# Sums of joined rows in a sandwich of attention and four expert layers: how many there are, and between which instructions they stand

## The reference

```
x = x + LN(attn(LN(x)))       # causal linear attention, 16 heads
x = x + LN(ffn(LN(x)))        # four layers, each as follows
  logits = x @ rw + rb ; the two best of 4 experts, gates that sum to 1
  xe = xhat * g[e] + b[e]     # xhat: x normalized; g, b per expert
  h  = gelu(xe @ w1[e] + b1[e]);  y = h @ w2[e] + b2[e]
  x  = sum over the two experts of gate * (x + y)
```

## Time and profile before

| | |
|---|---|
| median of three runs | 1641.62 us |
| profiled execution | 1646.7 us, its span 1644.9 us |
| PE busy | 1418.8 us (86%) |
| DVE busy | 1274.0 us (77%) |
| ACT busy | 1120.4 us (68%) |
| POOL busy | 847.8 us (52%) |
| attention stage | up to about 403 us |
| layers 0, 1, 2, 3 begin on DVE at | 422, 716, 1017, 1313 us |
| `joined_sums`, L1505 | 100 instructions, 77.8 us |

### The profile page before, as it was taken

The page is one execution under the profiler, slowest core; times in us unless marked ns, Lnnn a source line. Parts: engine busy times, 40 slices in busy tenths (PEclk is TensorE's granted clock), DMA queues, the critical chain, the costliest instruction groups (busy, mean ns, idle before and its releaser), DMA issues.

```text
span 1644.9 us, 36942 instructions
## 1 busy us (share of the span) xinstructions
PE 1418.8 (86%) x11037; PEld 1110.8 (68%) x11037; DVE 1274.0 (77%) x3803; ACT 1120.4 (68%) x1975; POOL 847.8 (52%) x1534
## 2 busy tenths in 40 slices
PE   6999989997779989887999888899989888888882
PEld 4666566667658877666787666678777666766661
DVE  6987888894478887878887877887887888676773
ACT  4443443440858988666898866688988668999871
POOL 2256566765745564234556513355652337787345
PEclk9998998995889999989999998999999899999986
DMA  7963666612858766545786754478766446876532
GB/s 285 397 228 129 260 236 236 269 31 56 222 154 247 229 223 185 179 134 175 208 262 204 216 184 135 131 232 258 233 209 190 141 140 189 206 206 170 168 64 20
DMA packets 181110, 314.11 MB, mean 191 GB/s; under 512 B 37569, under 2 KB 117809, under 8 KB 180529
## 3 DMA queue, kind: packets, MB, share of 16 engines
q1 hardware_dynamic: 159408, 288.27, 55.2%
q0 software_dynamic: 21504, 23.48, 6.2%
HBM read 205.20 MB, written 113.72 MB: 194 GB/s over the span
## 4 chain that ended last, share of the span: by engine, by line
PE 38%; DVE 14%; issue 13%; ACT 7%; POOL 3%; POOLq 0%; ACTq 0%; DVEq 0%
PE ps_h L1817 5%; PE ps_h L1819 5%; PE ps_h L1818 5%; PE ps_q L1850 5%; PE ps_y L1831 5%; PE ps_y L1833 5%; PE ps_y L1832 5%; ACT xh L1373 3%; DVE row L1505 3%; ACT hh L1395 2%; DVE hl L1468 2%; PE ps_t L1804 1%; DVE pbn L1474 1%; DVE row L1533 1%; PE ps_q L1848 1%
## 5 line engine op out<-in xcount | busy, mean ns | idle before, releaser
L1389 ACT ACTIVATE hg<-ps_h,bb 128x512 f32<-128x512 f32 x592 | 389.1, 684 | 225.4 <-PE ps_h L1819 224.4
L1468 DVE TENSOR_TENSOR hl<-hg,hh 128x1024 fp32r<-128x1024 f32 x296 | 360.6, 1220 | 200.2 <-ACT hh L1395 200.0
L1395 ACT ACTIVATE hh<-hg 128x1024 fp32r<-128x1024 f32 x296 | 313.1, 1058 | 3.3 <-PE ps_y L1833 0.9
L1303 POOL DMA_INDIRECT regions<-nrow,posi x192 | 228.9, 1192 | 85.3 <-issue 48.0
L1817 PE MATMUL ps_h<-xTh,w1b 128*128 128x512 f32 x592 | 261.9, 442 | 8.4 <-ACT hg L1389 7.0
L1819 PE MATMUL ps_h<-xTh,w1b 128*128 128x512 f32 x592 | 239.2, 404 | 0.0
L1818 PE MATMUL ps_h<-xTl,w1b 128*128 128x512 f32 x592 | 238.9, 403 | 0.0
L1831 PE MATMUL ps_y<-hh,w2b 128*128 128x512 f32 x592 | 238.8, 403 | 0.0
L1832 PE MATMUL ps_y<-hl,w2b 128*128 128x512 f32 x592 | 236.7, 400 | 0.0
L1833 PE MATMUL ps_y<-hh,w2b 128*128 128x512 f32 x592 | 236.7, 400 | 0.0
L1850 PE MATMUL ps_q<-ir,yb 128*128 128x140 f32 (+2 forms) x888 | 145.6, 298 | 102.0 <-DVE base L1576 61.9
(11 more groups left out here) (277 smaller groups left out, 2652.2 us busy)
## 6 DMA issues: line engine op xcount, KB each, us to landing
w1b<-w_split SPq DMA_DIRECT2D x148, 512.0 KB, 3.7
w2b<-w_split SPq DMA_DIRECT2D x148, 512.0 KB, 4.4
regions<-zero SPq DMA_DIRECT2D x14, 4326.0 KB, 24.6
row<-regions SPq DMA_DIRECT2D x84, 294.0 KB, 4.3
w_split<-wst SPq DMA_DIRECT2D x32, 512.0 KB, 5.1
wr<-in_L_ffn_w_dram SPq DMA_DIRECT2D x32, 256.0 KB, 4.9
regions<-regions SPq DMA_DIRECT2D x24, 294.0 KB
x<-in_L_attn_x_dram SPq DMA_DIRECT2D x16, 256.0 KB, 3.7
```

Source lines behind the costliest of these rows:

```text
L1303: g.indirect_dma_start(out=regions[layer % 2], out_offset=bass.IndirectOffsetOnAxis(ap=posi[r % 2][:, b:b + 1], axis=0), in_=nrow[r % 2][: ...
L1389: a.activation(hg[c // 2 % PAIRS][:, c % 2 * TILE:(c % 2 + 1) * TILE], ps_h[c % BANKS][:], ACT.Gelu, bias=bb[h % BBUFS][:, c % FC:c % FC + ...
L1395: a.activation(hh[j % PAIRS][:], hg[j % PAIRS][:], ACT.Identity).then_inc(hi, 1)
L1468: v.tensor_tensor(hl[n][:], hg[n][:], hh[n][:].bitcast(F32), ALU.subtract).then_inc(lo, 1)
```

## The change

Four edits.

1. `joined_sums` becomes `joined_sum`, one sum at a time, and a tile p takes sums only of the joins q up to p: 15 for a layer in place of 25. `SUM_AT` gives the pair of the layer at which each stands. `update` computes no shares any more: `shares_by_class` stands one pair before it (pair e+3 for tiles with sums).
2. The tables stand further apart: `early_counts` in pair e+9 and `early_tiles` in e+11 of tile 10. In layers 1 to 3 the late ones stand in pairs 9, 11, 13, 15 and 17, in layer 0 in 10, 12, 14, 16 and 18.
3. The folds go on through rounds 7 to 10 with the four experts of layer 1, and POOL adds their `b1` in round 12 (`second_biases`). `later_biases` is left with layers 2 and 3, 32 matmuls.
4. At the end of the attention stage DVE's addition of the later biases stands behind `make_u`, not before it.

```
+SUMS = [(p, q) for p in range(NX) for q in range(p + 1)]
+SUM_AT = [57, 59, 61, 63, 65, 65, 67, 69, 69, 71, 73, 73, 75, 77, 77]
-                return t - 3 if 3 <= t < 3 + E else None
+                return t - 3 if 3 <= t < 3 + 2 * E else None
+                def second_biases():
+                    pool.wait_ge(s_b1x, 2 * E)
+                    g.tensor_tensor(bst[:, E:2 * E, 0:FC], b1x[:, E:], cols[:, K:2 * K].rearrange("p (e c) -> p e c", c=FC), ALU.add).then_inc(s_bias, 1)
...
+                    if t == 12:
+                        second_biases()
...
+                make_u(NT - 1, 3 * NT - 1)
                 dve.wait_ge(s_b1late_ps, 1)
-                v.tensor_tensor(bst[:, E:, 0:FC], ps_b1[:, 0:(L - 1) * K].rearrange("p (n c) -> p n c", c=FC),
-                                cols[:, K:L * K].rearrange("p (n c) -> p n c", c=FC), ALU.add).then_inc(s_bias, 1)
-                make_u(NT - 1, 3 * NT - 1)
+                v.tensor_tensor(bst[:, 2 * E:, 0:FC], ps_b1[:, 0:(L - 2) * K].rearrange("p (n c) -> p n c", c=FC),
+                                cols[:, 2 * K:L * K].rearrange("p (n c) -> p n c", c=FC), ALU.add).then_inc(s_bias, 1)
...
                         pe.wait_ge(s_w1, 16)
+                        if e >= E:
+                            pe.wait_ge(s_w1all, (L - 1) * 16)
+                        weights, at = (w1s, e * F) if e < E else (w1all, (e - E) * F)
...
                 rows_T(NT)
-                later_biases(1)
                 project(NT - 1)
...
-                sp.wait_ge(s_bias, 3)
+                sp.wait_ge(s_bias, 4)
...
-                    dve.wait_ge(t_share, shares[0])
-
-                def joined_sums(n):
+
+                def joined_sum(n, q):

                     p, cols_ = PLACE[n] - FULL, width(n)
-                    dve.wait_ge(p_xh, n + 1)
-                    dve.wait_ge(upd, ROUND0[n])
+                    if q == 0:
+                        dve.wait_ge(p_xh, n + 1)
+                    dve.wait_ge(upd, ROUND0[layer(n) * NU + FULL + q + 1])
+                    link(dve)
                     r = row[n % ROWBUFS]
-                    for q in range(NX):
-                        chained(v.scalar_tensor_tensor(r[:, :, 0:cols_], joined[q][:, :, 0:cols_], belongs[:, q, p:p + 1], r[:, :, 0:cols_], ALU.mult, ALU.add))
-                        link(dve)
+                    chained(v.scalar_tensor_tensor(r[:, :, 0:cols_], joined[q][:, :, 0:cols_], belongs[:, q, p:p + 1], r[:, :, 0:cols_], ALU.mult, ALU.add))
...
                     if part == 0 and gathered(n):
-                        shares_by_class(n)
-                        if main(n):
-                            joined_sums(n)
+                        dve.wait_ge(t_share, shares[0])
+                        link(dve)
...
-                        late = j - START[l * NU] // 2 - (8 if l else 10)
+                        late = j - START[l * NU] // 2 - (9 if l else 10)
...
+                    for l in range(L):
+                        for (tile, q), at in zip(SUMS, SUM_AT):
+                            if at == j - START[l * NU] // 2:
+                                joined_sum(l * NU + FULL + NX + tile, q)
+                    n = ENDS.get(2 * (j - 3))
+                    if main(n) and gathered(n):
+                        shares_by_class(n)
+                    n = ENDS.get(2 * (j - 4))
+                    if joins_in(n if n is not None else -1):
+                        shares_by_class(n)
```

More of the change, by code:

```diff
@@ L93, in sandwich_kernel @@
         base, base_early = sb("base", [P, CL]), sb("base_early", [P, CL])
-        bst, b1x = sb("bst", [P, L * E, FC + 1]), sb("b1x", [P, E, FC])
+        bst, b1x = sb("bst", [P, L * E, FC + 1]), sb("b1x", [P, 2 * E, FC])
         arow = [sb(f"arow{q}", [P, NB, W]) for q in range(AROWS)]
@@ L499, in numbers_and_classes @@
                     g.tensor_copy(base[:], first_row[:]).then_inc(s_consts, 1)
+                def second_biases():
+                    pool.wait_ge(s_b1x, 2 * E)
+                    g.tensor_tensor(bst[:, E:2 * E, 0:FC], b1x[:, E:], cols[:, K:2 * K].rearrange("p (e c) -> p e c", c=FC), ALU.add).then_inc(s_bias, 1)
                 def first_biases():
                     pool.wait_ge(s_b1x, E)
-                    g.tensor_tensor(bst[:, 0:E, 0:FC], b1x[:], cols[:, 0:K].rearrange("p (e c) -> p e c", c=FC), ALU.add).then_inc(s_bias, 1)
+                    g.tensor_tensor(bst[:, 0:E, 0:FC], b1x[:, 0:E], cols[:, 0:K].rearrange("p (e c) -> p e c", c=FC), ALU.add).then_inc(s_bias, 1)
                     g.tensor_copy(bst[:, :, FC:FC + 1], cols[:, B2:B2 + L * E].unsqueeze(2)).then_inc(s_bias, 1)
@@ L816, in transposes @@
                     wait(pe, z_cnt, t - 3)
-                    wait(pe, s_b1x, min(max(t - 3, 0), E))
+                    wait(pe, s_b1x, min(max(t - 3, 0), 2 * E))
                     for b in range(NB):
@@ L859, in logits_and_counts @@
                         pe.wait_ge(s_w1, 16)
+                        if e >= E:
+                            pe.wait_ge(s_w1all, (L - 1) * 16)
+                        weights, at = (w1s, e * F) if e < E else (w1all, (e - E) * F)
                         for c in range(FC):
-                            last = mm(ps_a[:, FOLD.start + c:FOLD.start + c + 1], w1s[:, e * F + c * P:e * F + (c + 1) * P],
+                            last = mm(ps_a[:, FOLD.start + c:FOLD.start + c + 1], weights[:, at + c * P:at + (c + 1) * P],
                                       cols[:, LNB + e:LNB + e + 1], start=True, stop=True)
@@ L865, in later_biases @@
                 def later_biases(l):
-                    if l == 1:
-                        pe.wait_ge(s_w1all, (L - 1) * 16)
+                    if l == 2:
                         pe.wait_ge(a_s, NT * 8)
@@ L872, in later_biases @@
                             at = (n - E) * F + c * P
-                            last = mm(ps_b1[:, (n - E) * FC + c:(n - E) * FC + c + 1], w1all[:, at:at + P],
+                            last = mm(ps_b1[:, (n - 2 * E) * FC + c:(n - 2 * E) * FC + c + 1], w1all[:, at:at + P],
                                       cols[:, LNB + n:LNB + n + 1], start=True, stop=True)
@@ L1730, in _ @@
                         x_rest(n)
-                    if routed(m) and PLACE[m] == EARLY_FROM - 1:
-                        dve.wait_ge(t_base, tile_of(m) + NT + 1)
+                    early = ENDS.get(2 * (j - 9))
+                    if routed(early) and PLACE[early] == EARLY_FROM - 1:
+                        dve.wait_ge(t_base, tile_of(early) + NT + 1)
                         early_counts(dve, base)
-                    early = ENDS.get(2 * (j - 9))
+                    early = ENDS.get(2 * (j - 11))
                     if routed(early) and PLACE[early] == EARLY_FROM - 1:
@@ L1742, in _ @@
                             late_tiles(l)
-                        if late == 1:
+                        if late == 2:
                             joins_of_tiles(l)
-                        if late == 2:
+                        if late == 4:
                             row_parts()
-                        if late == 3:
+                        if late == 6:
                             row_values(0)
-                        if late == 4:
+                        if late == 8:
                             row_values(1)
```

## The result

Four runs of the changed kernel took 1571.57 to 1577.36 us, median 1576.9; four of the kernel before 1640.12 to 1646.62, median 1643.71. The ratio is 0.9587, 95% interval 0.9557 to 0.9618. The profiled execution has a span of 1574.6 us, 70.3 shorter than before. In this table a stretch runs from DVE's `hl` of one pair to that of another, and the last column is the term on record.

What follows compares the result with a forecast made beforehand. Bound: PE's products, with DVE's sums on the path in a loop of PE and DVE. Terms 54.3 - 5.7 + 6.6 + 1.7 + 6.8 - 10 = 53.7 us off 1646.7 gave 1593.0; less 5.1, 1588 us (8 in 10: 1564 to 1612).

Steps and rivals of the forecast that it cites:

- sums: Tiles with sums, layers 0 to 2: each should take 15.67 us, winning 54.3 us together.
- clock: Pauses left on PE in tiles with sums, layers 0 to 2: a third lower the granted clock, 5.7 us lost.
- layer 3: Tiles with sums of the last layer, plain loop 14.35 us: 6.6 us won, bounds zero to 10.
- tables: Table instructions moved to other pairs: 0.57 us won in each of three layers, 1.7 us.
- attention: Attention stage: 10 us lost by four folds in rounds 7 to 10, 6.8 us won at its end.
- The loop: A tile: PE's second part, 4.87 us to DVE's `hl`, 8.73 us on DVE, next second part; 13.60 us when plain.
- the second stretch: DVE's work from `hl` of pair e+6 to PE's next second part, 8.73 us; additions lengthen the tile by their whole size.
- the rest: DVE's 2.31 us wait for ACT's `hh` before `hl` of pair e+6; work added before that `hl` falls into it.
- The rival in which the sums vanish: Tiles with sums, layers 0 to 2: unseen slack makes five tiles take 13.60 us each, about 1557 us; chance 0.15.
- the first rival: Tiles with sums, layers 0 to 2: clock falls at all 12 remaining pauses, 1.43 us each, about 1599 us; chance 0.18.
- The step that only `row_part` changes sides: Tables: only `row_part`, 0.65 us long, moves from the second stretch to the rest; 0.57 us won in each of three layers.
- The step on the end: End of attention: later bias products start sooner and DVE's last rows lie beside them; 6.8 us won, between 1.1 and 7.9.

## Why the prediction was right, and where it was off

*The sum of the terms.* 53.7 us were predicted, and the profiled spans lie 70.3 apart. Taken as in the table above, all terms erred to the same side: sums 1.3, clock 5.7, layer 3 4.7, tables 1.7, attention 3.2, together 16.6. That the forecast of 1588 missed the median by 11 us and not by 16.5 is luck: it took off 5.1 us because before's profiled execution lay so far above the median, and the changed kernel's lay 0.4 below it. The 1576.9 also lies a little below 1578, the lower end that the forecast gave for its own mechanism.

*The sums* (54.3 predicted, 55.6 measured). The loop was right in its parts: the second stretch counts whole, the rest hides. Three kernels that had only the count, the place or the position within the loop changed came out at 1601, 1597 and 1561 for the 1598, 1592 and 1559 to 1563 worked out from it. The rival in which the sums vanish fails on the loops of 15.55 us in place of 13.60 and on the 1.75 us that PE still pauses.

*The clock* (5.7 us lost predicted, nothing measured in these tiles). This step failed on the length of the pause: "2.07 + 0.52 = 2.6 us". The 0.52 stood before one of the three plain second parts of the earlier trace rows only. The loop of 13.60 that the sum starts from ended at 821.65 without a pause, so the step should have given 2.07; 1.75 was measured, twelve times between 1.69 and 1.76, and the clock stayed at 1.00. So the first rival, by which all twelve would pay, does not hold for these pauses. At pauses near 2.6, which I had in mind, four of ten were followed by a longer loop in the kernel with 25 single sums, and the clock fell at three of three in the kernel with blocks.

*Layer 3* (6.6 predicted, 11.3 measured, above my upper bound of 10). I took its plain loop of 14.35 us as the floor of the tiles with sums. But pairs 60 to 72 lasted 12.2, 12.8 and 13.0 us for each four, less than a plain tile, where they had lasted 15.9, 16.0 and 16.8: 10.7 us. From pair 60 to the end the kernels with fifteen sums in blocks, fifteen singly and none take 83.4, 83.3 and 82.3 us, so between these neither place nor number matters there (in the rests they take 84.3, as said). The term also left out the clock: in these twelve pairs it was granted at 0.89, 0.93 and 0.91 before and at 1.00 since, and how much of the 10.7 us that is was not separated. Why these tiles are shorter than plain ones was not tried either; PE and ACT were busy for 35.9 and 35.8 of their 37.9 us, which leaves little time in which they could have waited for DVE.

*Tables* (1.7 predicted; 3.4 between the two profiles, 5 by the kernel with the old places). The step that only `row_part` changes sides, for a gain in each of layers 1 to 3, failed, and the figure came near by luck. In pairs 8 to 20, where the late tables stand, the changed kernel is 0.6 us shorter in layer 0, 1.0 longer in layer 1 and in layer 2, and 3.1 shorter in layer 3; the rest lies in later pairs, which vary. Before, the late counts (4.7 us) and the joins (2.6) both stood between PE's second part and the `hl` that follows DVE's rest, which came 9.43 us behind that part (758.57 to 768.00) in place of 4.87. Now the counts alone stand there (7.64 us, 739.48 to 747.12), and the joins went to the second stretch. At a full clock that gains: pairs 8 to 20 of layer 1 took 48.35 us in the kernel without sums and 49.82 in the one before. But in the changed kernel they hold a pause of 3.48 us, the clock fell at it, and they took 50.87:

```profile
758.51 1.70 PE L1868 MATMUL ps_q<-ir,yb 128*128 128x136 f32 x6 [3.48 <-DVE base L1583]
...
757.00:768.00 11.00, 9.49 (x35) 8.01 (x36) 7.83 (x27) 6.41 (x12) 5.83 (x10) 0.69 0.44 131
```

So the changed kernel does pay for the clock, at a place where the prediction had put no price.

*Attention* (-3.2 predicted, 0 in the profiled pair). By the landmarks above the folds cost about 9 (10 predicted, 4.1 to 12.4; some 4 by the kernel without the bias of layer 1) and the end won 4.9 (6.8 predicted, 1.1 to 7.9): about -4, and the two runs with the folds as before took 2.0 and 5.0 us less, each within the intervals. The step on the end failed where it named only PE and DVE; POOL's closing wait was late next.

Of the checks on record, the distances of the second parts and the `hl` that still waits for ACT came as stated, and the first load came within 5 us of before's. The pause did not, nor did the 15 to 16 us between the last counts on PE and the first load: they were 17.6 (386.68 to 404.32), as POOL's closing wait came last.

## What to carry to other kernels

Where an engine's loop has a rest at a known place, ask of each added instruction on which side of the rest it stands: here dropping ten sums of 25 was worth 45 us (1646.2 to 1601.1), and placing the other fifteen in the rests 41 more (to 1560.6). A stall's price in clock is to be read at several pauses of the same length, not at one longer pause. A stage whose start moves by several us from run to run needs landmarks within it, in several profiles; one pair of traces made two real terms look like nothing.

## What the runs showed of the hardware that was not expected

POOL's closing wait at the end of the attention stage took 5.27 or 5.28 us in every one of the 13 profiles, with folds or without.

The attention stage, the same instructions each time, varied by 7 us between nine profiles, and the time went with the granted clock. The nine rounds between the fourth and the thirteenth counts took 212.5 to 212.7 us where it was 0.92, 213.1 at 0.91, about 215.7 at 0.90 and 219.3 at 0.88.

Equal pauses did not act alike. One layer of the kernel with 25 single sums had three of 2.64 to 2.66 us: at the first two the clock stayed at 1.00, at the third it fell (0.90 over the 14 us behind it). The pause of 3.48 us in the tables of layer 1 lowered the clock in the changed kernel; in the kernel without sums one of 3.45 us at the same place left it at 1.00.
